# Cross-attention of a decoder layer: block transposes on VectorE with a trip through device memory in place of TensorE's transposes

## The chip, the cores and the metric

One NeuronCore of a Trainium2 chip runs the whole program. The metric is device time in microseconds from launch to end, the median of the runs. TensorE is called PE, VectorE DVE, ScalarE ACT, GpSimd POOL; SyncE (SP) only issues DMAs here.

## The reference

A decoder layer over 8 batch rows of 128 positions and 512 features, all in float32: causal self-attention, cross-attention and a linear layer, each with a residual and a layer norm ahead of it. The change touches the cross-attention, for each batch row b (the linear layer follows it row by row):

```python
kv = jnp.concatenate([context, latents], axis=1)          # 256 rows, 512 wide
q = latents @ Wq      # 32 heads of 128
k = kv @ Wk           # 8 heads of 128
v = kv @ Wv
q, k = rms_norm(q, q_norm_w), rms_norm(k, k_norm_w)
scores = einsum('bhgqd,bhkd->bhgqk', qg, k) / sqrt(128)   # four query heads to a key head
out = einsum('bhgqk,bhkd->bhgqd', softmax(scores), v)
return out @ Wo
```

The linear layer's weights come as 4-bit values with a scale per group and are unpacked on the chip.

## The kernel before

Products are made in float32r from split operands: a value is a high part (`hi`, rounded) plus a low part (`lo`, the rest), and `split_matmuls` (L76) issues three matmuls (hi x hi, lo x hi, hi x lo) for each block of 128 in the contraction. So every operand of a product needs a copy (mostly on ACT) for its high part and a subtraction (mostly on DVE) for its low part.

First comes `self_attention`, to about 249 us of the span. It leaves the rows in `x` (the accumulator `acc`), their normalised transposes `xT`, the context's transposes `cT`, the first set of weights, and the products of the first step in `ps_kv` and `ps_q`. `cross_attention_and_linear` then runs 64 steps s = 8 j + b: for each of the 8 key heads j (with its four query heads) the 8 batch rows b. The order of the work is written out by hand as one list for each engine, with semaphores between them. The bodies of j = 0 and j = 7 are written out, those between are a hardware loop.

A step does this. PE: `scores` (12 matmuls of 256 columns into `ps_s0`, `ps_s1`); `project_keys_values` for the next step (24 of 256 into `ps_kv`); `project_queries` for the next step (12 of 512 into `ps_q`); `probs_transposed` (8 transposes of 128x128 of p, L1210, into two banks `ps_pT`); `queries_keys_transposed` for the next step (4 transposes into `ps_q`, L1216, and 2 into `ps_kv`, L1221); `project_output` of the step before (12 of 512 into `ps_y`); `values` (6 of 512 into `ps_o`). DVE: the maxima over the scores and the bias of the exponential (`biases`), the scaling of p by the inverse of its total (`probs`, L1055), `v_lo`, the normalised keys `k_sb`, the low parts `pT_lo` (two), `qT_lo`, `kT_lo`, `oT_lo`, and the residual. ACT: four exponentials with their totals, the sums of squares for both rms norms, a copy `q_sb` of the queries, and the high parts. The rms of the queries isn't applied to them but to the scores, as the scale of the exponential. POOL: the two chains that turn sums of squares into inverse roots (`rms`, L882 and L884), and the low parts of the weights (`weights_low`, L876).

Weights of a key head: `wkv`, `wq` and `wo`, one buffer each for the raw array, the high and the low part. The high and low parts of the next head's `wkv` and `wq` are made in step b = 6, once the products of this head are issued, those of `wo` in b = 0. SP loads the raw arrays as they come free.

PSUM's eight banks are all in use: two for scores, two for the transposes of p, and `ps_q`, `ps_kv`, `ps_o`, `ps_y`. After the last step the linear layer's rows follow, each with statistics, norm, transposes, product and store.

## Time and profile before

| | |
|---|---|
| Median of 3 runs | 1114.6 us (1114.39 to 1115.09) |
| Profiled execution, its own time | 1114.33 us |
| Its span | 1112.2 us |
| Mean granted PE clock over the span | 0.982 of full speed |
| Busy in the span | PE 1050.4, DVE 757.1, ACT 611.9, POOL 358.5 us |
| DMA | 31.73 MB moved, mean 29 GB/s |
| First and last scores of the cross-attention | 253.7 and 1070.9 us |

The span runs from the first to the last instruction that the profiler recorded. Matmuls are pipelined, so the mean of one (395 ns for 512 columns) is longer than the distance at which they follow each other; the chain of waits shows that distance. Busy times of engines run side by side and don't add up.

### The profile page before, as it was taken

To read this page: it belongs to the slowest core of one execution; us is meant where nothing else is said; L and a number is where in the kernel's file an instruction comes from. 1 tells how busy PE (TensorE), PEld (TensorE's weight loads), DVE (VectorE), ACT (ScalarE), POOL (GpSimd) and SP (SyncE) were. 2 spreads that over 40 slices of the span, in tenths; PEclk is the share of its full clock that TensorE was granted. 3 is DMA by queue.
4 is the path that set the end of the run, shared out by engine and by line. 5 is a ranking of instruction groups with operands and counts; after the bars stand their busy time and mean duration, and the time that the engine had idled before them with its cause. 6 is when DMAs were issued, how large, how long until landed. Compare 5 with 4: busy or idle time off the path is not lost.

```text
span 1112.2 us, 19358 instructions
## 1 busy us (share of the span) xinstructions
PE 1050.4 (94%) x6436; PEld 902.8 (81%) x6436; DVE 757.1 (68%) x1561; ACT 611.9 (55%) x2324; POOL 358.5 (32%) x460
## 2 busy tenths in 40 slices
PE   6788888778999999999999999999999999999998
PEld 5666666547888888888888888888888888888886
DVE  6788888756557756665666576657666665667774
ACT  2666666525555655555555555555555555555551
POOL 4622333033114312431432143114313331433443
PEclk9899999878999999999999999999999999999999
DMA  5000010003001100110011011001100110010002
GB/s 180 21 10 9 9 66 10 1 3 126 6 1 58 39 1 2 57 38 0 19 38 38 0 57 38 0 0 57 38 0 0 57 38 0 11 37 1 1 1 76
DMA packets 8935, 31.73 MB, mean 29 GB/s; under 512 B 1600, under 2 KB 1600, under 8 KB 6720
## 3 DMA queue, kind: packets, MB, share of 16 engines
q1 hardware_dynamic: 8896, 31.23, 8.0%
q8 instruction: 22, 0.36, 0.1%
q14 instruction: 17, 0.14, 0.0%
HBM read 29.13 MB, written 2.10 MB: 28 GB/s over the span
## 4 chain that ended last, share of the span: by engine, by line
PE 64%; POOL 7%; DVE 3%; ACT 2%; issue 1%; POOLq 0%; DVEq 0%
PE ps_q L76 15%; PE ps_y L76 14%; PE ps_kv L76 13%; PE ps_s L76 7%; PE ps_o L76 7%; PE ps_pT L1210 4%; POOL wq_lo L876 3%; POOL wkv_lo L876 2%; PE ps_q L1216 2%; ACT p L957 1%; PE ps_kv L1221 1%; POOL q_rms L884 1%; DVE neg_max L1042 1%; POOL k_rms L884 1%; DVE wkv_hi L1035 0%
## 5 line engine op out<-in xcount | busy, mean ns | idle before, releaser
L957 ACT ACTIVATE p<-ps_s,bias,q_rms 128x256 f32<-128x256 f32 x256 | 141.3, 560 | 117.1 <-DVE bias L1046 116.3
L1068 DVE TENSOR_TENSOR pT_lo<-ps_pT,pT_hi 128x512 fp32r<-128x512 f32 x128 | 82.5, 686 | 75.6 <-ACT pT_hi L983 75.4
L993 ACT ACTIVATE oT_hi<-ps_o 128x512 fp32r<-128x512 f32 x64 | 38.3, 598 | 139.2 <-PE ps_o L76 139.2
L882 POOL TENSOR_TENSOR k_rms<-k_mean,rms_eps 128x2 f32<-128x2 f32 x64 | 19.6, 306 | 283.9 <-ACT k_squares L964 283.9
L76 PE MATMUL ps_y<-wo_hi,oT_hi 128*128 128x512 f32 x256 | 106.5, 416 | 0.0
L76 PE MATMUL ps_q<-wq_hi,xT_hi 128*128 128x512 f32 x256 | 101.1, 395 | 2.5 <-POOL wq_lo L876 2.5
L76 PE MATMUL ps_q<-wq_hi,xT_lo 128*128 128x512 f32 x256 | 101.9, 398 | 0.0
L76 PE MATMUL ps_y<-wo_hi,oT_lo 128*128 128x512 f32 x256 | 101.4, 396 | 0.0
L76 PE MATMUL ps_q<-wq_lo,xT_hi 128*128 128x512 f32 x256 | 100.9, 394 | 0.0
L76 PE MATMUL ps_y<-wo_lo,oT_hi 128*128 128x512 f32 x256 | 100.7, 393 | 0.0
L971 ACT ACTIVATE q_sb<-ps_q 128x512 f32<-128x512 f32 x64 | 38.3, 599 | 100.8 <-PE ps_q L76 99.5
L882 POOL TENSOR_TENSOR q_rms<-q_mean,rms_eps 128x4 f32<-128x4 f32 x64 | 13.5, 210 | 245.2 <-ACT q_squares L976 245.2
L1085 DVE TENSOR_TENSOR oT_lo<-ps_o,oT_hi 128x512 fp32r<-128x512 f32 x64 | 44.2, 691 | 69.3 <-ACT oT_hi L993 69.3
L1055 DVE TENSOR_SCALAR p<-p,inv 128x256 f32<-128x256 f32 x256 | 86.5, 380 | 4.5
L1042 DVE TENSOR_REDUCE neg_max<-ps_s 128x2 f32<-128x512 f32 x128 | 87.5, 684 | 2.2 <-PE ps_s L76 2.2
L1081 DVE TENSOR_TENSOR x<-ps_y,x 128x512 f32<-128x512 f32 x64 | 44.3, 691 | 62.3 <-PE ps_y L76 62.3
L976 ACT ACTIVATE q_squares<-q_sb 128x128 f32<-128x128 f32 x256 | 77.3, 334 | 0.0
L76 PE MATMUL ps_s<-kT_hi,qT_hi 128*128 128x256 f32 x256 | 72.7, 284 | 1.2 <-DVE kT_lo L1076 1.2
L76 PE MATMUL ps_kv<-wkv_lo,cT_hi 128*128 128x256 f32 x256 | 73.4, 287 | 0.0
L76 PE MATMUL ps_kv<-wkv_hi,cT_lo 128*128 128x256 f32 x256 | 73.2, 286 | 0.0
L76 PE MATMUL ps_kv<-wkv_hi,cT_hi 128*128 128x256 f32 x256 | 73.0, 285 | 0.0
L76 PE MATMUL ps_s<-kT_hi,qT_lo 128*128 128x256 f32 x256 | 72.7, 284 | 0.0
(210 smaller groups left out, 3316.1 us busy)
## 6 DMA issues: line engine op xcount, KB each, us to landing
raw_wq<-in_x_wq SPq DMA_DIRECT2D x8, 1024.0 KB, 4.8
raw_wo<-in_x_wo SPq DMA_DIRECT2D x8, 1024.0 KB, 4.9
raw_wkv<-in_x_wkv SPq DMA_DIRECT2D x8, 512.0 KB, 3.3
ctx_raw<-in_ctxT SPq DMA_DIRECT2D x8, 256.0 KB, 2.6
out<-raw_wq SPq DMA_DIRECT2D x8, 256.0 KB, 2.0
x<-in_x SPq DMA_DIRECT2D x1, 1536.0 KB, 9.8
raw_wq<-in_a_wq SPq DMA_DIRECT2D x2, 512.0 KB, 6.0
raw_wq<-in_a_wo SPq DMA_DIRECT2D x1, 1024.0 KB, 4.7
```

What stands on the lines that cost most here:

```text
L76: mm = pe.matmul(out, lhsT, rhs, start=start and i == 0, stop=stop and i == len(terms) - 1)
L876: i = pool.tensor_tensor(w[1][:, c, :], raw[:, c, :], f32(w[0][:, c, :]), ALU.subtract)
L957: act.activation(p[:, g, :], ps_s[g // 2][:, g % 2 * KV:(g % 2 + 1) * KV], ACT.Exp, bias=bias[:, g:g + 1], scale=q_rms[:, g:g + 1], accum_ ...
L971: act.activation(q_sb[:], ps_q[:].rearrange("p (g d) -> p g d", g=XG), ACT.Copy).then_inc(q_ok, 1)
L976: i = act.activation(q_squares[:, g, :], q_sb[:, g, :], ACT.Square, scale=XD ** -0.5, accum_out=q_mean[:, g:g + 1])
L993: act.activation(oT[0][:], ps_o[:].rearrange("p (g s) -> p g s", g=XG), ACT.Copy).then_inc(o_hi, 1)
L1042: dve.tensor_reduce(neg_max[:, two], ps_s[h][:].rearrange("p (g k) -> p g k", g=2), AX.X, ALU.max, negate=True).then_inc(max_ok, 1)
L1055: i = dve.tensor_scalar(p[:, g, :], p[:, g, :], inv[:, g:g + 1], None, ALU.mult)
L1068: dve.tensor_tensor(pT[1][:, t], ps_pT[t][:].rearrange("p (g s) -> p g s", g=XG), f32(pT[0][:, t]), ALU.subtract).then_inc(pT_lo, 1)
L1081: dve.tensor_tensor(acc[:, b, :], ps_y[:], acc[:, b, :], ALU.add).then_inc(acc_ok, 1)
L1085: dve.tensor_tensor(oT[1][:], ps_o[:].rearrange("p (g s) -> p g s", g=XG), f32(oT[0][:]), ALU.subtract).then_inc(o_lo, 1)
L1210: mm = pe.transpose(ps_pT[t][:, g * S:(g + 1) * S], p[:, g, t * S:(t + 1) * S], ident[:])
```

## The change

The 14 transposes of a step leave PE. For p, for the raw queries and for the normalised keys there is instead:

1. `dve.transpose`, which transposes each 32x32 block and leaves the blocks where they are put (`p_blocks`, 1024 columns in two instructions; `qk_blocks`, 768 columns in two: the queries straight from `ps_q`, the keys from `k_sb`);
2. one DMA on SP's queue that stores the blocks to a scratch array in device memory (512 KB for p, 384 KB for queries and keys), with a wait for it;
3. four DMAs that load them back, each into 32 partitions (a quadrant j of the transposed array), in runs of 1024 bytes for p and 768 for queries and keys (`pT_raw`, `qk_raw`). The scratch arrays are double, as is `pT_raw`; `p_blocks`, `qk_blocks` and `qk_raw` are single.

High and low parts are made from these arrays in SBUF: `pT_hi` and `qT_hi`, `kT_hi` on ACT; `pT_lo` (in place, one instruction of 1024 columns) and `qT_lo` on POOL; `kT_lo` on DVE. The copy `q_sb` is gone: the squares are read from `ps_q`, and the arrays of squares are bf16 now.

The pipeline is deeper: in iteration s PE issues the scores of s, the keys, values and queries of s + 2, the output of s - 2 and the values of s - 1, in this order. `v` has four buffers, `q_rms` four. The other engines' lists follow. All 64 steps are written out; there is no hardware loop.

`wq` and `wkv` (high and low) are double, so the next head's are made earlier: `wkv_hi` at b = 0, `wo_hi` at 1, `wq_hi` at 2 on DVE; the low parts on POOL in pieces of two blocks at b = 2, 3 (`wkv`), 4, 5 (`wq`) and 1 (half of `wo`; DVE makes the other half). The first set of `wq` serves as the linear layer's weights. The linear layer has two banks of its own (`ps_xn`, `ps_f`, those of `ps_pT`) and starts in the last two iterations: its rows 0 to 3 are issued there, the rest between the last products.

The core of the diff:

```diff
-        wq, wkv, wo = mem["wq"], mem["wkv"], split("wo", [P, XG, D])
+        wq = [mem["wq"], split("wq1", [P, C, D])]
+        wkv = [mem["wkv"], split("wkv1", [P, C, NKV])]
+        wo = split("wo", [P, XG, D])
...
+        qk_blocks = sb("qk_blocks", [P, 4, XG + 2, R])
+        qk_raw = sb("qk_raw", [P, 4, XG + 2, R])
...
-        v = [split(f"v{i}", [P, 2, XD]) for i in range(2)]
+        v = [split(f"v{i}", [P, 2, XD]) for i in range(4)]
...
-        pT = split("pT", [P, 2, XG, S])
+        p_blocks = sb("p_blocks", [P, 8, XG, R])
+        pT_hi_sb = sb("pT_hi_sb", [P, 4, 2, XG * R], F32R)
+        pT_raw = [sb(f"pT_raw{i}", [P, 4, 2, XG * R], F32R) for i in range(2)]
...
+            def queries_keys(s):
+                sp.wait_ge(k_blocked, s + 1)
+                sp.wait_ge(q_blocked, s + 1)
+                wait(sp, qT_lo, s)
+                scratch = io["qk_scratch"][s % 2]
+                sp.dma_start(scratch, qk_blocks[:].rearrange("p j x c -> p (j x c)")).then_inc(qk_stored, 16)
+                wait(sp, kT_lo, s)
+                sp.wait_ge(qk_stored, 16 * (s + 1))
+                quadrants = scratch.rearrange("(i r) (j x) -> j r i x", i=4, j=4)
+                for j in range(4):
+                    sp.dma_start(qk_raw[R * j:R * j + R].rearrange("p i x c -> p i (x c)"), quadrants[j]).then_inc(qk_loaded[s % 4], 16)
+            def probs(s):
+                sp.wait_ge(p_blocked, 2 * s + 2)
+                if s >= 2:
+                    sp.wait_ge(pT_lo, s - 1)
+                scratch = io["p_scratch"][s % 2]
+                sp.dma_start(scratch, p_blocks[:].rearrange("p m g c -> p (m g c)")).then_inc(p_stored, 16)
+                if s >= 2:
+                    sp.wait_ge(o_ps, s - 1)
+                sp.wait_ge(p_stored, 16 * (s + 1))
+                quadrants = scratch.rearrange("(i r) (j x) -> j r i x", i=4, j=4)
+                for j in range(4):
+                    sp.dma_start(f32(pT_raw[s % 2][R * j:R * j + R].rearrange("p i t x -> p i (t x)")),
+                                 quadrants[j]).then_inc(p_loaded[s % 4], 16)
...
+            for s in range(STEPS):
+                j, b = divmod(s, B)
+                if s + 1 < STEPS:
+                    queries_keys(s + 1)
+                probs(s)
+                if b == 3 and j < LAST:
+                    sp.wait_ge(wo_lo, j + 1)
+                    sp.wait_ge(wo_lo_dve, j + 1)
+                    load(raw_wo, "x_wo", wo_in, j + 1)
+                if b == 4 and j + 2 < XKVH:
+                    sp.wait_ge(wkv_lo, 2 * j + 2)
+                    load(raw_wkv, "x_wkv", wkv_in, j + 2)
+                if b == 6 and j + 2 < XKVH:
+                    sp.wait_ge(wq_lo, 2 * j + 2)
+                    load(raw_wq, "x_wq", wq_in, j + 2)
...
+            def queries_low(s):
+                pool.wait_ge(qT_hi, s + 1)
+                pool.tensor_tensor(qT[1][:].rearrange("p g (i c) -> p g i c", i=4),
+                                   qk_raw[:, :, 0:XG, :].rearrange("p i g c -> p g i c"),
+                                   f32(qT[0][:]).rearrange("p g (i c) -> p g i c", i=4), ALU.subtract).then_inc(qT_lo, 1)
+
+            def probs_low(s):
+                pool.wait_ge(pT_hi, s + 1)
+                raw = pT_raw[s % 2][:].rearrange("p i t x -> p (i t x)")
+                pool.tensor_tensor(raw, f32(raw), f32(pT_hi_sb[:].rearrange("p i t x -> p (i t x)")),
+                                   ALU.subtract).then_inc(pT_lo, 1)
...
+            for s in range(STEPS):
+                j, b = divmod(s, B)
+                if j < LAST and b in (2, 3):
+                    weights_low(wkv[(j + 1) % 2], raw_wkv, (2 * b - 4, 2 * b - 3), wkv_hi, wkv_lo, j + 1)
+                if j < LAST and b in (4, 5):
+                    weights_low(wq[(j + 1) % 2], raw_wq, (2 * b - 8, 2 * b - 7), wq_hi, wq_lo, j + 1)
+                if s:
+                    probs_low(s - 1)
+                if s + 2 < STEPS:
+                    k_rms_step(s + 2)
+                if s + 1 < STEPS:
+                    queries_low(s + 1)
+                if b == 1:
+                    weights_low(wo, raw_wo, (2, 3), wo_hi, wo_lo, j + 1)
+                if s + 2 < STEPS:
+                    q_rms_step(s + 2)
+                if j == LAST:
...
             def probs_high(s):
-                for t in range(2):
-                    act.wait_ge(pT_ps, 2 * s + t + 1)
-                    act.activation(pT[0][:, t], ps_pT[t][:].rearrange("p (g s) -> p g s", g=XG), ACT.Copy).then_inc(pT_hi, 1)
+                act.wait_ge(p_loaded[s % 4], landed(s))
+                act.activation(pT_hi_sb[:], f32(pT_raw[s % 2][:]), ACT.Copy).then_inc(pT_hi, 1)

             def queries_keys_high(s):
-                act.wait_ge(qT_ps, s + 1)
-                act.activation(qT[0][:], ps_q[:].rearrange("p (g d) -> p g d", g=XG), ACT.Copy).then_inc(qT_hi, 1)
-                act.wait_ge(kT_ps, s + 1)
-                act.activation(kT[0][:], ps_kv[:, 0:KV], ACT.Copy, scale=key_scale[:, 0:1]).then_inc(kT_hi, 1)
+                act.wait_ge(qk_loaded[s % 4], landed(s))
+                act.activation(kT[0][:].rearrange("p (i t c) -> p i t c", i=4, t=2), qk_raw[:, :, XG:, :], ACT.Copy,
+                               scale=key_scale[:, 0:1]).then_inc(kT_hi, 1)
+                act.activation(qT[0][:].rearrange("p g (i c) -> p g i c", i=4),
+                               qk_raw[:, :, 0:XG, :].rearrange("p i g c -> p g i c"), ACT.Copy).then_inc(qT_hi, 1)

...
+            keys_values(0)
+            query_sums(0)
+            keys_values(1)
+            query_sums(1)
+            queries_keys_high(0)
+            for s in range(STEPS):
+                j, b = divmod(s, B)
+                if s >= 2:
+                    output_high(s - 2)
                 exps(s)
...
+                if s:
+                    probs_high(s - 1)
+                if s + 2 < STEPS:
+                    keys_values(s + 2)
+                if s + 1 < STEPS:
                     queries_keys_high(s + 1)
...
+                if s + 2 < STEPS:
+                    query_sums(s + 2)
...
+            def probs(s, h):
+                two = slice(2 * h, 2 * h + 2)
+                dve.wait_ge(exp_done, 2 * s + h + 1)
+                dve.reciprocal(inv[:, two], total[:, two]).then_inc(inv_ok, 1)
+                dve.wait_ge(inv_ok, 2 * s + h + 1)
+                for g in range(2 * h, 2 * h + 2):
+                    i = dve.tensor_scalar(p[:, g, :], p[:, g, :], inv[:, g:g + 1], None, ALU.mult)
+                i.then_inc(p_ok, 1)
+                wait(dve, p_stored, 16 * s)
+                dve.wait_ge(p_ok, 2 * s + h + 1)
+                dve.transpose(p_blocks[:, :, two, :], p[:, two, :].rearrange("p g (m r) -> p m g r", r=R)).then_inc(p_blocked, 1)
...
+            def keys_blocked(s):
                 dve.wait_ge(k_rms_ok, s + 1)
                 dve.tensor_tensor(k_sb[:], kv_rows[:, :, 0:XD], k_rms[:].unsqueeze(2).broadcast_to([P, 2, XD]),
                                   ALU.mult).then_inc(k_ok, 1)
...
+                wait(dve, qk_stored, 16 * s)
+                dve.wait_ge(k_ok, s + 1)
+                dve.transpose(qk_blocks[:, :, XG:, :].rearrange("p j x c -> p x j c"),
+                              k_sb[:].rearrange("p t (j r) -> p t j r", r=R)).then_inc(k_blocked, 1)
...
+            def queries_blocked(s):
+                dve.wait_ge(q_ps, s + 1)
+                wait(dve, qk_stored, 16 * s)
+                dve.transpose(qk_blocks[:, :, 0:XG, :].rearrange("p j x c -> p x j c"),
+                              ps_q[:].rearrange("p (g j r) -> p g j r", g=XG, r=R)).then_inc(q_blocked, 1)
...
+            def keys_low(s):
                 dve.wait_ge(kT_hi, s + 1)
+                dve.scalar_tensor_tensor(kT[1][:].rearrange("p (i t c) -> p i t c", i=4, t=2), qk_raw[:, :, XG:, :],
+                                         key_scale[:, 0:1], f32(kT[0][:]).rearrange("p (i t c) -> p i t c", i=4, t=2),
+                                         ALU.mult, ALU.subtract).then_inc(kT_lo, 1)
...
+            for s in range(2):
+                queries_blocked(s)
+                values_low(s)
+                keys_blocked(s)
+            keys_low(0)
+            for s in range(STEPS):
+                j, b = divmod(s, B)
                 biases(s)
...
+                if s >= 2:
+                    output_low(s - 2)
+                probs(s, 0)
+                probs(s, 1)
+                if s + 2 < STEPS:
+                    values_low(s + 2)
+                if s + 1 < STEPS:
+                    keys_low(s + 1)
+                if s + 2 < STEPS:
+                    keys_blocked(s + 2)
+                    queries_blocked(s + 2)
+                if s >= 2:
+                    residual(s - 2)
+                if b == 1:
+                    output_weights(j)
+                if j < LAST and b == 0:
+                    weights_high(wkv[(j + 1) % 2], raw_wkv, wkv_in, j + 1, wkv_hi)
+                if j < LAST and b == 2:
+                    weights_high(wq[(j + 1) % 2], raw_wq, wq_in, j + 1, wq_hi)
...
+            def values(s):
+                pe.wait_ge(pT_lo, s + 1)
+                wait(pe, o_lo, s)
+                hi, lo = pT_hi_sb, pT_raw[s % 2]
+                split_matmuls(pe, ps_o[:], [(v[s % 4][0][:, t, :], v[s % 4][1][:, t, :], hi[:, :, t, :], lo[:, :, t, :])
+                                            for t in range(2)]).then_inc(o_ps, 1)
+
...
+            project_keys_values(1)
+            project_queries(1)
+            for s in range(STEPS):
+                j, b = divmod(s, B)
...
                 scores(s)
...
+                if s + 2 < STEPS:
+                    project_keys_values(s + 2)
...
+                if s + 2 < STEPS:
+                    project_queries(s + 2)
+                if s >= 2:
+                    project_output(s - 2)
...
+                if s:
+                    values(s - 1)
+            xn_transposed(4)
...
-    nc = bacc.Bacc("TRN2", target_bir_lowering=False, num_devices=1)
+    nc = bacc.Bacc("TRN2", target_bir_lowering=False, num_devices=1, dynamic_dma_scratch_size=4096)
...
+    io["p_scratch"] = [nc.dram_tensor(f"p_scratch{i}", (P, XG * KV), F32, kind="Internal").ap() for i in range(2)]
+    io["qk_scratch"] = [nc.dram_tensor(f"qk_scratch{i}", (P, (XG + 2) * XD), F32, kind="Internal").ap() for i in range(2)]
```

## Rows read from the trace of the kernel before

**Rows 1.** Window table: us, busy (instructions) per engine, granted PE clock, DMA share, GB/s.

```profile
400.00:450.00 50.00, 50.00 (x310) 44.15 (x309) 30.70 (x72) 28.57 (x108) 14.34 (x22) 1.00 0.03 12
```

**Rows 2.** Chain of waits, one step: start us, us, engine, tile, line, instructions.

```profile
410.20 1.42 PE ps_s L76 x12
411.62 2.88 PE ps_kv L76 x24
414.50 2.80 PE ps_q L76 x12
417.30 0.87 PE ps_pT L1210 x8
418.18 0.47 PE ps_q L1216 x4
418.65 0.22 PE ps_kv L1221 x2
418.87 2.79 PE ps_y L76 x12
421.66 1.40 PE ps_o L76 x6
```

**Rows 3.** Waits: engine line <- releaser: us in total, times, longest.

```profile
PE ps_q L76 <- POOL wq_lo L876: 2.5, 7, 0.4
```

**Rows 4.** Chain of waits, start of the cross-attention and end of the program.

```profile
251.25 0.44 DVE k_sb L1062
...
253.66 2.90 PE ps_s L76 x12
...
1085.80 2.82 PE ps_y L76 x12
...
1109.01 0.69 DVE raw_wq L1130
```

**Rows 5.** DMA issues of the page (KB each, us to landing); SP's timeline (start, us).

```profile
raw_wq<-in_x_wq SPq DMA_DIRECT2D x8, 1024.0 KB, 4.8
...
raw_wkv<-in_x_wkv SPq DMA_DIRECT2D x8, 512.0 KB, 3.3
...
out<-raw_wq SPq DMA_DIRECT2D x8, 256.0 KB, 2.0
...
447.22 0.33 SPq L840 DMA_DIRECT2D raw_wkv<-in_x_wkv  x1
```

**Rows 6.** Groups by line: shapes, count | busy us, mean ns | idle before, releaser.

```profile
L1042 DVE TENSOR_REDUCE neg_max<-ps_s 128x2 f32<-128x512 f32 x128 | 87.5, 684 | 2.2 <-PE ps_s L76 2.2
L1055 DVE TENSOR_SCALAR p<-p,inv 128x256 f32<-128x256 f32 x256 | 86.5, 380 | 4.5
L1068 DVE TENSOR_TENSOR pT_lo<-ps_pT,pT_hi 128x512 fp32r<-128x512 f32 x128 | 82.5, 686 | 75.6 <-ACT pT_hi L983 75.4
L1046 DVE TENSOR_TENSOR bias<-neg_max,q_rms 128x2 f32<-128x2 f32 x128 | 44.7, 349 | 4.9
...
L1035 DVE CAST wq_hi<-raw_wq 128x2048 fp32r<-128x2048 f32 x7 | 8.6, 1227 | 0.0
...
L957 ACT ACTIVATE p<-ps_s,bias,q_rms 128x256 f32<-128x256 f32 x256 | 141.3, 560 | 117.1 <-DVE bias L1046 116.3
```

**Rows 7.** Timeline of VectorE and GpSimd around a weight switch: start us, us, instruction.

```profile
448.26 5.02 POOL L876 TENSOR_TENSOR wq_lo<-raw_wq,wq_hi 128x512 fp32r<-128x512 f32 x4
450.77 1.29 DVE L1046 TENSOR_TENSOR bias<-neg_max,q_rms 128x2 f32<-128x2 f32 x1
...
464.31 0.16 DVE L1046 TENSOR_TENSOR bias<-neg_max,q_rms 128x2 f32<-128x2 f32 x1
```

**Rows 8.** Groups of GpSimd by line, columns as in rows 6.

```profile
L884 POOL TENSOR_TENSOR q_rms<-q_rms,minus_half 128x4 f32<-128x4 f32 x64 | 64.4, 1007 | 5.0
...
L876 POOL TENSOR_TENSOR wkv_lo<-raw_wkv,wkv_hi 128x256 fp32r<-128x256 f32 x28 | 26.9, 988 | 8.0 <-DVE wkv_hi L1035 8.0
...
L927 POOL TENSOR_TENSOR f_w_lo<-raw_wo,f_w_hi 128x1024 fp32r<-128x1024 f32 x2 | 4.8, 2404 | 0.0
```

More of the change, by code:

```diff
@@ L1174, in _, with project_keys_values @@
+            statistics(6)
+            normalised(6)
+            out_row(4)
+            out_row(5)
+            output_low(STEPS - 1)
+            xn_low_row(6)
+            residual(STEPS - 1)
+            statistics(7)
+            normalised(7)
+            out_row(6)
+            xn_low_row(7)
+            out_row(7)
         @block.tensor
         def _(pe):
[L1176 to L1180 removed]
+            def project_keys_values(s):
+                j, b = divmod(s, B)
+                wait(pe, v_lo, s)
+                wait(pe, k_ok, s)
+                wait(pe, wkv_lo, 2 * j)
+                rows, weight = slice(b * S, (b + 1) * S), wkv[j % 2]
```

443 lines of the change are left out of this document (180 added, 263 removed).

## The prediction, made before the changed kernel ran

> **What bounds the kernel now.** I read the window table first, then the chain of waits, then the groups of instructions by line. In the window table [rows 1] the reader sees TensorE (PE) busy for all of a 50 us stretch of the cross-attention at a granted clock of 1.00 (the 2.4 GHz level), beside VectorE (DVE) 30.7, ScalarE (ACT) 28.6 and GpSimd (POOL) 14.3 us, with the DMA engines almost idle. The chain in the same stretch [rows 2] is one head step of TensorE and nothing else: 1.42 + 2.88 + 2.80 + 0.87 + 0.47 + 0.22 + 2.79 + 1.40 = 12.85 us. So a step costs what TensorE issues in it, and there are 64. The reader should note the three short pieces (L1210, L1216, L1221): 14 transposes, 0.87 + 0.47 + 0.22 = 1.56 us per step. The self-attention before it, up to about 249 us, is not touched.
>
> **What the change takes off TensorE.** All 14 transposes: 64 x 1.56 = 99.8 us. The other 66 matmuls of a step stay as they are, 11.29 us. The second set of weights also removes the wait for the low half of the query weights, 2.5 us in 7 switches [rows 3]. The query product stands ahead of the output product in the old step too (414.50 and 418.87 in [rows 2]), so that order moves nothing; what moves is the distance: products for step s+2, values of s-1 and output of s-2 stand in step s now. TensorE's time is the same, and a result may be one step later before anyone waits.
>
> **Start.** Before, the normalised keys of step 0 are ready at 251.25 + 0.44 = 251.7 and the first scores start at 253.66 [rows 4]. After, between the two stand: a block transpose (0.4), a store of 384 KB, four loads, the high halves (two ACT instructions, about 1.1), the low half of the queries on POOL (1.29, priced below). The nearest DMAs [rows 5]: 256 KB stored 2.0 us, 512 KB loaded 3.3, 1024 KB loaded 4.8, so 1.5 us per further 512 KB. Estimate: store 2.0 + 0.4 = 2.4 plus the issue; the loads, issued one behind the other at 0.33 each, 3.3 at the least (as one load of 512 KB) and 1.0 + 4.8 = 5.8 at the most (from the last issue, at the price of twice the bytes, should loads into 32 partitions at a time run at half the rate). I take 4.2, near the lower end, since the bytes decide. The first scores come at about 262, 8.3 late; but the key/value and query products of step 1 (2.88 + 2.80) are done in that gap, so net +2.6. The first p needs its own trip, and the first two steps have nothing else to fill: about 5 us of gaps. **End.** After the last output product before, 1088.6, the chain runs to 1109.0 through five more rows of the linear layer [rows 4]; after the change those rows mostly stand ahead of it. They are moved, not removed; only the idle of the statistics chain, about 4 us, is partly filled: -1. Together -2.5 + 2.6 + 5 - 1 = +4.
>
> **The best case** is thus 1112.2 - 99.8 + 4 = 1016.4 of span; with the 2.1 us around it (the profiled execution took 1114.3) 1018.5. The median of the three shown, 1114.6, is 0.3 above that execution, which is nothing here.
>
> **What has to fit under 11.29 us a step.** Three loops come close to that, and each is priced by its nearest rows.
>
> *VectorE.* Per step [rows 6]: two maxima with their bias (2 x (0.68 + 0.16)), four scalings of p (4 x 0.38), two reciprocals (0.3), `oT_lo` and the residual (2 x 0.69), and three passes of 256, `v_lo`, `kT_lo` and `k_sb` (3 x 0.44, by `k_sb` in [rows 4]). Gone are `pT_lo` twice and `qT_lo`, 3 x 0.69 = 2.06. New are four block transposes: p twice 512 columns, queries 512, keys 256. No row shows one. A pass of 512 columns takes 0.68 in every form seen from PSUM and a fast scaling 0.38 for 256, so the bounds are about 0.4 and 1.4 (twice the pass) for 512; I take 0.68 and 0.42, the pass they are nearest to: 2.5 in all. Sum 8.7; with the weight copies (1.23 for 2048 columns: two of these, one of half the width and the new half subtraction come to about 0.5 as a mean over eight steps) 9.2 of 11.29, between 8.3 and 11.8. That fits, alone.
>
> The Trainium skill (page VectorE: DVE Perf Modes, section The three transpose paths) gives 311 ns for a 128x128 block transpose in bf16, and the 32x32 blocks only. Taken four times for 512 columns that would be 1.24 us and VectorE's sum 11.1 rather than 9.2; taken as a fixed part and one column per cycle it would be my value. No row here can tell which.
>
> *The port that VectorE and GpSimd share.* The row that speaks against this change is the bias of 128x2: 0.16 us in an ordinary step, and 1.29 at 450.77, while POOL is inside its group of four subtractions [rows 7]; it ended where one of these ended. Where POOL works from SBUF, the small instruction waits for it. In the new kernel POOL has such work in every step: `queries_low`, 512 columns, 1.29 us, and `probs_low`, 1024 columns in one instruction, 2.40 [rows 8]. With the two rms chains (2.2, of which the power for the queries alone is 1.01) and the low halves of the weights ((4 x 0.99 + 6 x 1.29)/8 = 1.5) POOL is busy for 7.4 us of a step, against 3.7 (14.34/50 of 12.85) now. `probs_low` starts when ACT has made `pT_hi`, right after the exponentials, just where VectorE scales the second half of p. If the last scaling waits for it, that costs up to 2.4; if `kT_lo`, now read from SBUF, meets `queries_low`, up to 1.3. VectorE's sum is then 12.9 at worst and 9.2 at best. VectorE has about 1.1 us per step of waits for the exponentials (560 ns each [rows 6]) and the rms that can overlap these, so I put its loop at 10.5 to 12.
>
> The Trainium skill (page SBUF — State Buffer, section Who interferes with whom) says that the pair is an exclusive lock held for the whole instruction. By that rule the 2.4 us instruction is worse than the four of 1.29 seen here, and a VectorE that always meets it is at 12.9.
>
> *SP and the trips.* SP waits for each store before it issues the loads, and both trips go through its one queue. Trip of p: 2.75 (store of 512 KB) + 4 x 0.33 = 4.1; trip of q and k: 2.4 + 1.3 = 3.7; 7.8 at the least. A store queued behind the loads before it waits for their bytes, up to 1.5 each, and the weights (2.5 MB in eight steps, 0.9 us per step) go through the same rings: 7.8 + 3.0 + 0.9 = 11.7 at the most. I take 10. The traffic, 1.8 MB per step, is about 160 GB/s plus the weights. As latency: p blocked about 6.4 us into its step, its trip 2.75 + 0.33 + 4.2 = 7.3, ready 13.7 after the scores started; ACT takes it up in the next step after that step's exponentials, at 15.3. So p has some 1.6 us of slack, the keys and queries about 1.5.
>
> **Forecast.** The three loops lie close to TensorE's 11.29 and each has steps in which it is longer: weights on POOL in four of eight steps, copies on VectorE in three, loads of 1 MB or 512 KB ahead of a trip in three. I expect no stall in about half the steps and some 0.8 us in the others, 0.4 as a mean: 64 x 0.4 = 25. 1018 + 25 = **1043 us**, TensorE about 96% busy, a step of 11.7.
>
> **Rivals.** (1) *A loop binds, but below the old step.* The scalings wait for `probs_low` in nearly every step, or SP's queue is full: 12.2 us a step, 1018 + 64 x 0.9 = 1076 (1062 to 1105). For it: the 1.29 us bias row, and sums that reach 12.9 and 11.7. Against it: VectorE now has 19 us of waits in 50, and these waits can overlap. (2) *The other side: the round trip closes a loop longer than the old step.* From q blocked to `kT_hi` and on to the next q blocked stand store 2.75, loads 4.2, ACT 0.5 to 1.1, `kT_lo` 0.5, `k_sb` and its transpose 0.9, the q transpose 0.7: 9.6 to 10.2. If trips take 3.5 us more than I think (loads at the 5.8 end, and a store that waits behind them), this is 13.6 per step: 1018 + 64 x 2.3 = 1165, slower. It decides from 1.5 us of stall per step on ((1114.3 - 1018.5)/64), that is a step of 12.8. For it: nothing in the trace shows a load into 32 partitions in runs of 768 bytes. Against: slack in three places and a DMA share of 0.03 now. (3) *Nothing stalls*: 1018, if `probs_low` happens to fall into VectorE's waits. It differs from the forecast in size only.
>
> **How the numbers follow.** Forecast with rival 3 as its lower end (1012 to 1062): 0.53. Rival 1: 0.27. Rival 2: 0.17. Between them, within 0.2% of no change (2.2 us, about what a measurement of this kernel can tell): 0.03. So faster 0.80, same 0.03, slower 0.17. The range takes the first two whole, and leaves out rival 2: 1012 to 1105.
>
> **What will show it.** TensorE rows of steady steps: no transposes, a step of 11.3 where nothing stalls; wrong if the matmuls themselves became slower. The block transposes near 0.68 for 512 columns; at 1.2 VectorE binds. The mean of the p scaling (0.38 now) and of the bias (0.35 now) would rise with the port: over 0.8 for the scaling says rival 1. TensorE's waits by releaser: `qT_lo` or `kT_lo` ahead of the scores speak for the trip of q and k, `pT_lo` ahead of the values for that of p, `k_sb` or the blocked queries ahead of the products for VectorE. The forecast is wrong if a trip takes over 9 us from store to last load, or if VectorE's busy share comes over 90%.

## The result, and the profile after

The changed kernel takes 1168.3 us (median, 1165.5 to 1170.7) against 1114.5 for the kernel before on the same chip (1111.7 to 1115.1): ratio 1.049, 95% interval 1.046 to 1.052. It is slower by 54 us where 1043 was forecast.

The head of the page of the kernel after, with its chain of waits by share, and its DMA issues (KB each, us to landing):

```profile
span 1164.9 us, 18100 instructions
PE 991.7 (85%) x5523; PEld 835.0 (72%) x5540; DVE 863.9 (74%) x1633; ACT 577.3 (50%) x2196; POOL 573.8 (49%) x572
...
DVE 24%; DMA 21%; PE 14%; SPq 8%; issue 5%; POOL 3%; ACT 3%; DVEq 0%; POOLq 0%; ACTq 0%
...
p_scratch<-p_blocks SPq DMA_DIRECT2D x64, 512.0 KB, 2.6
pT_raw<-p_scratch SPq DMA_DIRECT2D x256, 128.0 KB, 3.0
qk_scratch<-qk_blocks SPq DMA_DIRECT2D x64, 384.0 KB, 3.5
qk_raw<-qk_scratch SPq DMA_DIRECT2D x256, 96.0 KB, 2.2
raw_wq<-in_x_wq SPq DMA_DIRECT2D x8, 1024.0 KB, 7.0
```

TensorE has 14% of the chain. VectorE, DMA and SP's queue (SPq) have 53% together. The window table answers to [rows 1] (us; busy time of PE, PEld, DVE, ACT, POOL; granted TensorE clock; DMA share; GB/s), here for the kernel after:

```profile
400.00:450.00 50.00, 43.99 (x239) 37.37 (x238) 40.48 (x73) 25.40 (x95) 31.07 (x33) 0.97 0.51 161
...
300.00:1000.00 700.00, 629.13 (x3512) 546.11 (x3513) 528.08 (x1038) 360.36 (x1334) 386.61 (x387) 0.95 0.53 166
```

TensorE stands still for 6 us in 50. Over 300 to 1000 us its granted clock is a mean of 0.95, where the kernel before had 1.00 (the 2.4 GHz level) in the same stretch. The groups that answer to [rows 6, 8] (mean ns of one behind the busy us):

```profile
L1132 DVE TENSOR_SCALAR p<-p,inv 128x256 f32<-128x256 f32 x256 | 157.9, 658 | 4.5
L940 POOL TENSOR_TENSOR pT_raw<-pT_raw,pT_hi_sb 128x1024 fp32r<-128x1024 f32 x64 | 157.4, 2459 | 157.4 <-ACT pT_hi_sb L1045 157.4
...
L1136 DVE STREAM_TRANSPOSE p_blocks<-p 128x512 f32<-128x512 f32 x128 | 91.1, 712 | 13.3
L1121 DVE TENSOR_REDUCE neg_max<-ps_s 128x2 f32<-128x512 f32 x128 | 87.8, 686 | 46.2 <-PE ps_s L76 45.9
...
L1159 DVE SCALAR_TENSOR_TENSOR kT_lo<-qk_raw,key_scale,kT_hi 128x256 fp32r<-128x256 f32 x64 | 45.7, 714 | 123.0 <-ACT kT_hi L1049 122.9
...
L1154 DVE STREAM_TRANSPOSE qk_blocks<-ps_q 128x512 f32<-128x512 f32 x64 | 43.3, 676 | 7.9 <-PE ps_q L76 7.4 <-PEq L88 0.3
...
L1124 DVE TENSOR_TENSOR bias<-neg_max,q_rms 128x2 f32<-128x2 f32 x128 | 40.6, 318 | 4.4
...
L1148 DVE STREAM_TRANSPOSE qk_blocks<-k_sb 128x256 f32<-128x256 f32 x64 | 28.5, 446 | 6.7
```

The block transposes cost what was put in. The same scaling of `p` takes 658 ns instead of 380.

**Where the time went.** The distance between the first maxima (`neg_max`) of one step and the next, read off VectorE's timeline, is the length of a step (64 steps in all, eight to a head); the place is `b`, the step's number within its head. The means over heads 1 to 6, in us:

```
place b           0      1      2      3      4      5      6      7     head
before        12.86  12.86  12.86  12.86  12.86  12.86  12.86  13.46    103.5
after         12.25  12.51  13.17  11.29  17.18  12.68  11.28  14.27    104.6
```

At places 3 and 6 a step is 11.28 to 11.29, TensorE's own work, as forecast. The rest stalls: 14.4 us a head over 8 x 11.28, 1.8 a step and not 0.4. So the 12.6 us that the transposes freed in each head are all spent. The 52.7 us by which the span grew divide so: the first maximum comes at 269.2 instead of 255.3 (+14); the seven heads 0 to 6 take 730.2 instead of 725.6 (+5); the last head's seven steps 112.9 instead of 91.7 (+21), one of them 25.6; from the last maximum to the end 52.6 instead of 39.7 (+13).

The 17.18 at place 4 in the chain of waits of the kernel after (start us, us, what):

```profile
523.57 2.62 DMA p_scratch<-p_blocks
...
528.08 0.38 SPq L844
...
528.56 8.65 DMA qk_scratch<-qk_blocks
...
538.59 2.47 DMA qk_raw<-qk_scratch
...
541.49 0.62 ACT qT_hi L1051
...
542.18 1.28 POOL qT_lo L933
...
543.50 2.93 PE ps_s L76 x12
```

L844 issues the 1 MB load of `raw_wo`; the 384 KB store of the blocked queries and keys is issued 0.48 us behind it and lands after 8.65 us. A step earlier (store at 515.70, first load behind it at 519.05) it took under 3.35. The store is late by 5.3 and the scores wait. So it is every time in the heads 0 to 6: from the store to the first of its loads back, SP needs 6.7 to 8.7 us behind each of the 13 loads of 1 MB and 5.4 to 5.9 behind each of the six of 512 KB. The waits of the engines say the same (line <- releaser: us in total, times, longest; kernel after):

```profile
ACT kT_hi L1049 <- DMA qk_raw<-qk_scratch: 170.7, 53, 9.0
...
PE ps_s L76 <- POOL qT_lo L933: 86.9, 37, 6.7
...
SPq L854 <- DMA qk_scratch<-qk_blocks: 265.7, 63, 8.3
```

The 12.3 to 13.2 of places 0 to 2 are in VectorE's list. Its chain, and GpSimd's and VectorE's timelines beside it (start us, us; kernel after):

```profile
505.85 0.63 DVE p L1132 x2
...
507.37 2.99 DVE p L1132 x2
...
511.47 1.22 DVE kT_lo L1159
```

```profile
507.74 2.45 POOL L940 TENSOR_TENSOR pT_raw<-pT_raw,pT_hi_sb 128x1024 fp32r<-128x1024 f32 x1
```

The first pair of scalings takes 0.63, the second 2.99, and it ends about when `probs_low` does (510.36 against 510.19).

### The profile page after: what moved, and what is told of

Read it like the earlier page. It is cut to its first block, busy times and chain, and to the rows that moved or that the text cites. A ratio compares the mean times of both kernels' runs of the same rounds, so it can differ in the third digit from the quotient of the medians.

```text
span 1164.9 us, 18100 instructions
## 1 busy us (share of the span) xinstructions
PE 991.7 (85%) x5523; PEld 835.0 (72%) x5540; DVE 863.9 (74%) x1633; ACT 577.3 (50%) x2196; POOL 573.8 (49%) x572
## 4 chain that ended last, share of the span: by engine, by line
DVE 24%; DMA 21%; PE 14%; SPq 8%; issue 5%; POOL 3%; ACT 3%; DVEq 0%; POOLq 0%; ACTq 0%
DMA qk_scratch<-qk_blocks 12%; DVE p L1132 8%; DMA p_scratch<-p_blocks 6%; PE ps_s L76 4%; SPq L871 4%; DMA qk_raw<-qk_scratch 3%; DVE p_blocks L1136 3%; DVE neg_max L1121 3%; PE ps_q L76 3%; SPq L857 3%; PE ps_kv L76 3%; PE ps_y L76 2%; DVE bias L1124 2%; POOL qT_lo L933 2%; DVE oT_lo L1170 1%
## 5 line engine op out<-in xcount | busy, mean ns | idle before, releaser
L940 POOL TENSOR_TENSOR pT_raw<-pT_raw,pT_hi_sb 128x1024 fp32r<-128x1024 f32 x64 | 157.4, 2459 | 157.4 <-ACT pT_hi_sb L1045 157.4
L1132 DVE TENSOR_SCALAR p<-p,inv 128x256 f32<-128x256 f32 x256 | 157.9, 658 | 4.5
L76 PE MATMUL ps_s<-kT_hi,qT_hi 128*128 128x256 f32 x256 | 81.9, 320 | 86.9 <-POOL qT_lo L933 86.9
L1039 ACT ACTIVATE q_squares<-ps_q 128x128 bf16<-128x128 f32 x256 | 67.4, 278 | 148.4 <-DVE qk_blocks L1154 148.4
L1159 DVE SCALAR_TENSOR_TENSOR kT_lo<-qk_raw,key_scale,kT_hi 128x256 fp32r<-128x256 f32 x64 | 45.7, 714 | 123.0 <-ACT kT_hi L1049 122.9
L933 POOL TENSOR_TENSOR qT_lo<-qk_raw,qT_hi 128x512 fp32r<-128x512 f32 x64 | 81.9, 1279 | 100.1 <-ACT qT_hi L1051 99.5
L76 PEld LDWEIGHTS ps_s<-kT_hi,qT_hi 128*128 128x128 f32 x256 | 53.7, 210 | 104.4 <-POOL qT_lo L933 103.1
L1049 ACT ACTIVATE kT_hi<-qk_raw,key_scale 128x256 fp32r<-128x256 f32 x64 | 32.7, 511 | 170.7 <-DMA qk_raw<-qk_scratch 170.7
L1136 DVE STREAM_TRANSPOSE p_blocks<-p 128x512 f32<-128x512 f32 x128 | 91.1, 712 | 13.3
L76 PE MATMUL ps_s<-kT_lo,qT_hi 128*128 128x256 f32 x256 | 77.8, 304 | 0.0
```

The source lines that it names most:

```text
L76: mm = pe.matmul(out, lhsT, rhs, start=start and i == 0, stop=stop and i == len(terms) - 1)
L933: pool.tensor_tensor(qT[1][:].rearrange("p g (i c) -> p g i c", i=4), qk_raw[:, :, 0:XG, :].rearrange("p i g c -> p g i c"), f32(qT[0][:]) ...
L940: pool.tensor_tensor(raw, f32(raw), f32(pT_hi_sb[:].rearrange("p i t x -> p (i t x)")), ALU.subtract).then_inc(pT_lo, 1)
L1039: i = act.activation(q_squares[:, g, :], ps_q[:, g * XD:(g + 1) * XD], ACT.Square, scale=XD ** -0.5, accum_out=q_mean[:, g:g + 1])
L1049: act.activation(kT[0][:].rearrange("p (i t c) -> p i t c", i=4, t=2), qk_raw[:, :, XG:, :], ACT.Copy, scale=key_scale[:, 0:1]).then_inc(k ...
L1132: i = dve.tensor_scalar(p[:, g, :], p[:, g, :], inv[:, g:g + 1], None, ALU.mult)
```

## The experiments

Each ratio is to the kernel before, whose runs were made beside it, with its 95% interval. "Places" are step lengths by `b` as above. Line numbers in fences are those of each kernel.

**What stalls the steps: the weights' loads, GpSimd, the end, the start.** Five kernels, each of which undoes one suspect.

`x1_light`: the weights of later heads are loaded as 16 numbers a partition; the rest of them stays that of an earlier head.

```diff
+            def load_light(raw, name, sem, j):
+                sp.dma_start(raw[:, 0, 0:16], io[name][j][:, 0:16]).then_inc(sem, 16)
...
-                    load(raw_wo, "x_wo", wo_in, j + 1)
+                    load_light(raw_wo, "x_wo", wo_in, j + 1)
```

(The other two loads likewise.)

> The weight loads of later heads are cut to 16 elements per partition (8 KB each), so later heads compute with stale weights; all waits, copies and low parts stay. Theory A (a 1 MB or 512 KB load issued right ahead of the store of queries and keys delays that trip): the three long steps of a head (17.2, 12.7 and 14.3 us in the changed kernel) fall to 11.3 to 11.8, 10 us per head, 7 heads: about 1098 us. Rival B (VectorE waits for GpSimd on the shared port): these loads were hidden, the steps stay, at most 10 us come back: 1158 or more. Rival C (each trip is too long by itself): the same as B.

Measured 1107.5, ratio 0.994 (0.991 to 0.997): 61 us less than after, where 70 was expected. Place 4 falls from 17.18 to 12.07, place 7 from 14.27 to 11.52; SP issues as many DMAs as before, so it is the bytes that cost and not the issues. The loads are the largest part; places 1 and 2 stay at 12.40 and 13.15.

`x2_split`: `probs_low` in four instructions of 256 columns.

```diff
-                pool.tensor_tensor(raw, f32(raw), f32(pT_hi_sb[:].rearrange("p i t x -> p (i t x)")),
-                                   ALU.subtract).then_inc(pT_lo, 1)
+                high = pT_hi_sb[:].rearrange("p i t x -> p (i t x)")
+                for c in range(4):
+                    part = slice(256 * c, 256 * (c + 1))
+                    i = pool.tensor_tensor(raw[:, part], f32(raw[:, part]), f32(high[:, part]), ALU.subtract)
+                i.then_inc(pT_lo, 1)
```

> The low part of p on GpSimd is made in four instructions of 256 columns in place of one of 1024. Theory B (port): the mean of the scaling of p falls from 0.66 to about 0.45 us and the steps b = 0, 1, 2 of a head, bound by VectorE, lose 0.5 to 1.5 us each: 15 to 30 us in all, 1138 to 1153 us; the last head, where the scaling waits 3 to 4 us, gives more. Theory A: the steps behind the weight loads stay long, 17.2 and 14.3. If the four instructions run back to back without letting VectorE in, nothing changes: 1168.

Measured 1144.3, ratio 1.028 (1.023 to 1.034), 24 less. The scaling in this kernel's groups:

```profile
L1135 DVE TENSOR_SCALAR p<-p,inv 128x256 f32<-128x256 f32 x256 | 116.6, 497 | 4.5
```

497 ns, between 380 and 658. At 505 us of its timeline a pair of scalings takes 1.10 beside GpSimd's group of four (2.98): VectorE waits for one piece, not for the group.

`x3_tail`: the first linear rows stand behind the last scores instead of ahead of them.

```diff
+                scores(s)
                 if j == LAST and b == 7:
+                    linear(0)
                     xn_transposed(2)
+                    linear(1)
                     xn_transposed(3)
-                scores(s)
...
-                    linear(2 * b - 12)
-                    linear(2 * b - 11)
+                    if b == 7:
+                        linear(2)
+                        linear(3)
```

> The first two rows of the linear layer and the transposes of rows 2 and 3 are issued behind the scores of the last step, not ahead of them. Theory D (the last scores wait for the chain of the norm, a step of 25.6 us): the scores of step 63 start 12 to 15 us earlier; part comes back because the linear rows are then late, so 6 to 12 us are gained: 1156 to 1162 us. Rival: the end is set by the last trip of p and the rows behind it in any case: 1168.

Measured 1155.1, ratio 1.039 (1.035 to 1.043), 13 less; the step of 25.6 falls to 16.8. The profiled execution took 1169.8, more than the other four (1152.8 to 1157.9), so its trace shows the step but not the gain: its last head is 10 us shorter and its heads 0 to 6 are 7 longer than in the kernel after.

`x4_start`: step 0's queries pass ahead of step 1's sums and rms, in ACT's, POOL's and VectorE's lists.

```diff
             keys_values(1)
+            queries_keys_high(0)
             query_sums(1)
-            queries_keys_high(0)
```

(ScalarE's list; the other two are changed to match.)

> At the start of the cross-attention the high and low parts of the queries of step 0 are made ahead of the sums of squares and the rms of step 1. Theory E (the first scores wait in GpSimd's and ScalarE's queues behind step 1, 267.4 in place of the 262 that I forecast): the first scores start 4 to 5 us earlier and all follows: 1164 us. Rival: the trip of step 1 then sets the pace and nothing is left of it: 1168.

Measured 1165.9, ratio 1.048 (1.041 to 1.055): nothing that can be told from after. The first maximum comes at 259.4 instead of 269.2; the maximum of step 8 is 6.4 ahead, that of step 16 only 2.4, and the last 2.4. An early start runs into the same loops, which give it back.

`x5_no_low`: the low part of `p` is made for 16 of its 1024 columns only.

```diff
-                pool.tensor_tensor(raw, f32(raw), f32(pT_hi_sb[:].rearrange("p i t x -> p (i t x)")),
-                                   ALU.subtract).then_inc(pT_lo, 1)
+                high = pT_hi_sb[:].rearrange("p i t x -> p (i t x)")
+                pool.tensor_tensor(raw[:, 0:16], f32(raw[:, 0:16]), f32(high[:, 0:16]), ALU.subtract).then_inc(pT_lo, 1)
```

> The changed kernel with the low part of p made for 16 of 1024 columns only, so the product of the values uses the full p as low part in the rest. Theory B (port): the scaling of p returns to 0.38 us, the steps b = 0 to 2 to the sum of VectorE's list, and more is gained than with the four instructions: 1130 to 1142 us. The steps behind the weight loads stay at 14 to 17 us, so it doesn't come below 1120.

Measured 1120.9, ratio 1.007 (1.004 to 1.010): 47 less, more than forecast. Places 0 to 2 are 11.92, 12.11 and 10.97, which gives back 2.9 of their 4.1 us over TensorE's work; places 4 and 7 stay at 16.32 and 13.92. The scaling is at 378 ns, its old 380 [rows 6], so the long instruction accounts for all of its rise. Twice x2's gain leaves room for something else that the instruction held up; `w4_order_only` below looks for it.

**Small pieces of weights.** `y1_pieces` loads the same bytes in 256 and 128 KB pieces, each behind the loads of queries and keys and ahead of the store of `p`. `y2_parts` is that with x2 and x3; `y3_spread` adds the spreading of the 16 scale loads over three steps; `y4_casts` adds the high halves of `wkv` and `wq` on ScalarE.

```diff
+                if b in (2, 3, 4, 5) and j < LAST:
+                    piece(raw_wo, "x_wo", wo_in, j + 1, b - 2)
...
                 probs(s)
...
-                    load(raw_wo, "x_wo", wo_in, j + 1)
```

> All the weights are loaded, in pieces of 256 or 128 KB spread over the steps, each issued behind the loads of queries and keys and ahead of the store of p. Theory A (it is the place and the size of a load in SP's queue, not the bytes, that costs): as with the tiny loads, 1100 to 1115 us, the steps b = 4, 5, 7 at 11.3 to 12.5. Rival F (the bytes cost wherever they stand, since the DMA engines are short): those steps share out the same loss, 1145 or more. Rival G: the store of p behind them is late and the values wait for p: PE waits for pT_lo ahead of ps_o of more than 20 us in all.

> The pieces, the low part of p in four instructions, and the linear rows behind the last scores, together. If the three losses are independent, about 60 + 24 + 11 us off 1168: 1065 to 1080, below the kernel before. If the port and the loads hide each other, 1090 to 1100.

> As y2_parts, and the 16 loads of the linear layer's scales, which SP issues in a row for 7.6 us between two trips, are spread over three steps. Theory A: the step of 18 us at the start of the last head falls to 12.5 to 13.5, 5 us less than y2_parts. Rival: no difference.

> As y3_spread, and ScalarE makes the high parts of wkv and wq in place of VectorE. Theory B (VectorE's list is what binds the steps b = 0, 1, 2): they lose 0.7 and 1.2 us, 7 heads: about 10 us less than y3_spread. Rival: ScalarE's copy of 2048 columns (about 2 us) delays the sums of squares and the exponentials, and nothing is gained.

```
                median   ratio (95%)                place 0 to 7
y1_pieces       1130.4   1.017 (1.013 to 1.020)     12.06 14.17 13.17 11.19 12.31 12.64 13.07 11.96
y2_parts        1110.7   0.998 (0.996 to 1.000)     12.17 14.22 12.33 10.96 11.97 12.40 12.77 12.11
y3_spread       1107.3   0.994 (0.992 to 0.997)     12.13 14.03 12.29 10.97 12.10 12.52 12.75 12.31
y4_casts        1106.1   0.994 (0.990 to 0.997)     11.86 14.28 11.49 11.62 12.46 12.68 12.52 12.35
```

The pieces give 38 of x1's 61. At places 4, 5 and 7 together they give 7.2 us a head, against 8.4 in x1; what they lack stands mostly at places 0, 1 and 6. The expectations of y1, y2 and y4 are missed. In y3 step 56 falls from 17.97 to 14.34, where 12.5 to 13.5 was expected. In y4 places 0 and 2 do lose 0.3 and 0.8, but places 3 to 5 grow by as much together, and in place of 10 us less there is 1, which can't be told from y3. So most steps stay near 12.3, whatever is taken off VectorE. In y4's chain of waits:

```profile
444.79 4.19 DMA p_scratch<-p_blocks
...
449.41 0.70 SPq L903
...
451.17 3.08 DMA qk_scratch<-qk_blocks
...
456.08 0.43 SPq L847
456.62 4.15 DMA p_scratch<-p_blocks
```

SP's own list is now the loop: store of `p`, wait, four loads (L903), store of queries and keys, wait, four loads, a piece (L847), the next store of `p` after 11.83 us. Behind the piece the store of `p` takes 4.2, where it took 2.6 in the kernel after. Place 1, at 14.0 to 14.3 in all four, is longer still: there y4's chain (474.58 to 493.88) leaves SP after the loads of queries and keys and goes through VectorE's list, with the copy `wo_hi` (1.14) in it.

**SP's order.** `z1_swap` is y4 with the two trips beside each other in SP's list: store of `p`, store of q and k, loads of `p`, loads of q and k. `z2_swap_only` is the changed kernel with that swap alone, `z3_swap_y3` is y3 with it.

```diff
                     queries_keys(s + 1)
+                if s:
+                    load_probs(s - 1)
+                if s + 1 < STEPS:
+                    load_queries_keys(s + 1)
                 probs(s)
```

(`queries_keys` and `probs` issue only their stores now.)

> As y4_casts, and SP issues the store of the next queries and keys ahead of the loads of p, so the store no longer queues behind their bytes and its latency lies beside their issue. Theory H (in y4_casts SP's own list is what binds: store of p 4.2, four issues 1.75, store of q and k 3.3, four issues 1.75, a piece 0.45: 11.5 to 11.9 us a step): SP's list shrinks to about 10 us, steps of 11.5 on the mean, 1070 to 1085 us. Rival (VectorE binds): the steps stay near 12.3, 1100 or more.

> The changed kernel with this exchange in SP's list alone. Here the big weight loads still stand ahead of the trips, behind the loads of p and ahead of nothing else: theory A, extended: a weight load now stands ahead of the store of p and no longer ahead of that of q and k... the load follows the loads of q and k, so the long steps 17.2 and 14.3 become 12 to 14: about 1120 to 1140 us. Rival H alone: a gain of at most 1 us per step in the short steps, 1150 or more.

> As z1_swap with the weight copies on VectorE (y3_spread and the exchange). Theory H: 1075 to 1090 us; z1_swap is lower by 5 to 10 us once SP no longer binds, since then VectorE's list does in the steps b = 0 and 2.

z1 1137.1 (1.024, 1.021 to 1.026), z2 1130.9 (1.018, 1.015 to 1.021), z3 1130.8 (1.017, 1.015 to 1.020). The swap takes some 35 off the changed kernel (0.031 of 1114) and *adds* about 32 to y4 (0.030), where 1070 to 1085 was expected; z3 was expected at 1075 to 1090.

z2's time is as expected, and its profile shows why the loads cost so much in the kernel after. The weights are still loaded whole there and still stand ahead of the store of queries and keys (the expectation says otherwise), but SP now issues them right behind the store of `p` and not behind its loads back, so 4.1 to 6.5 us ahead of the store of queries and keys instead of 0.5:

```profile
505.96 0.38 SPq L844 DMA_DIRECT2D raw_wo<-in_x_wo  x1
510.73 0.32 SPq L852 DMA_DIRECT2D qk_scratch<-qk_blocks  x1
...
513.35 1.73 SPq L860 DMA_DIRECT2D qk_raw<-qk_scratch  x4
```

The store has landed after 2.62 at most. Over the 19 such stores of the heads 0 to 6 it is 2.6 to 4.4, where it was 5.4 to 8.7. The places are 12.59, 14.11, 13.14, 11.37, 12.64, 12.30, 12.33 and 12.06: the long steps at 4 and 7 are gone with every byte and every whole load still there. So it is the distance between load and store that decides. Some 0.7 of the difference is the swap's own: its stores no longer stand right behind the loads of `p`, and their median falls from 3.3 in x1, which has no weights to wait for either, to 2.6.

What the swap costs, one turn of z1's chain of waits shows:

```profile
506.64 3.92 DMA pT_raw<-p_scratch
...
510.58 1.07 ACT pT_hi_sb L1074
...
511.72 3.01 POOL pT_raw L969 x4
...
514.96 0.71 POOL k_rms L949
515.69 0.44 DVE k_sb L1181
...
516.59 0.69 DVE qk_blocks L1191
...
517.33 0.32 SPq L884
...
519.24 4.68 DMA pT_raw<-p_scratch
```

The loads of `p` now wait for the blocked queries and keys, those for `k_rms`, and `k_rms` stands behind the low part of `p` in GpSimd's list, which needs the loads of `p`. A loop of 12.4 to 13.3 us. The same loop is in z2's chain.

**GpSimd's and ScalarE's order.** The keys' squares ahead of `pT_hi` on ScalarE, `k_rms` ahead of the low part of `p` on GpSimd: in y4 (`w1_order`), in z1 (`w2_order_swap`), in the changed kernel alone (`w4_order_only`); `w3_wo_late` is w2 with `q_rms` ahead of GpSimd's half of `wo_lo`.

```diff
+                if s + 2 < STEPS:
+                    k_rms_step(s + 2)
                 if s:
                     probs_low(s - 1)
-                if s + 2 < STEPS:
-                    k_rms_step(s + 2)
```

(GpSimd's list; on ScalarE `keys_values(s + 2)` likewise goes ahead of `probs_high(s - 1)`.)

> As y4_casts, with the sums of squares and the rms of the keys ahead of the high and low part of p in ScalarE's and GpSimd's lists. Theory H (SP's own list binds y4_casts): little changes, 1098 to 1106 us. Theory K (the loop over the low part of p and k_rms binds): 1070 to 1085.

> As z1_swap (1137 us) with that order. Theory K: the loop loads of p, pT_hi, low part, k_rms, k_sb, blocked queries, store is cut; both SP's list (10 us) and VectorE's are then below 12: 1065 to 1085 us, the best so far. Theory H has nothing to say against it. If VectorE still binds: 1100 or more.

> As w2_order_swap, with the rms of the queries ahead of GpSimd's half of the output weights. The step b = 1 (14.9 us in z1_swap) loses 1 to 2 us if that half delayed the chain: 7 to 14 us less than w2_order_swap. Rival: nothing, since that rms is needed two steps later.

> The changed kernel with the new order alone. The weight loads, the port and the end are as they were, so theories A and B leave 1155 to 1165 us; theory K would give 1140 or less.

```
                median   ratio (95%)                place 0 to 7
w1_order        1104.3   0.992 (0.989 to 0.995)
w2_order_swap   1060.7   0.953 (0.951 to 0.955)     11.35 12.26 11.62 11.59 11.44 11.41 11.28 11.43
w3_wo_late      1060.0   0.953 (0.951 to 0.955)
w4_order_only   1129.4   1.014 (1.011 to 1.017)     12.12 12.50 11.86 10.52 15.65 12.96 11.30 13.76
```

In w1 the order changes nothing that can be told from y4: SP's list is the loop there (in its chain over 450 to 500 us the two stores and SP's issues of the loads have 74%). In w2, where the swap has taken that away, the same order is worth some 78 us against z1 (0.071 of 1114); and the swap, which cost 32 in y4, is worth 44 against w1. In the changed kernel alone the order is worth 39 (1129.4, where the expectation was 1155 to 1165); w4's group

```profile
L1132 DVE TENSOR_SCALAR p<-p,inv 128x256 f32<-128x256 f32 x256 | 89.1, 390 | 4.5
```

is back at 390 ns: behind `k_rms`, the low part of `p` no longer meets the scalings (it meets `kT_lo` instead, 1175 ns against 714, where VectorE has idle time). So w4 does two things at once, it lets `k_rms` pass and keeps GpSimd's long instruction off the scalings, and no run here separates them. x2, which lets VectorE in and keeps the order, gave 24; what w4 and x5 gave beyond that can be the order's or the rest of the port's (in x2 a pair of scalings still takes 1.10 instead of 0.63). w3 finds nothing in `wo_lo`, where 7 to 14 was expected.

w2 beats both kernels: 1060.7, 50 below the 1111.0 of the original beside it. Its window table:

```profile
500.00:550.00 50.00, 49.60 (x299) 43.67 (x298) 37.33 (x85) 30.54 (x111) 31.27 (x41) 1.00 0.72 200
...
300.00:1000.00 700.00, 681.41 (x3941) 591.42 (x3940) 534.75 (x1167) 434.12 (x1512) 478.74 (x623) 1.00 0.64 184
```

TensorE is busy again at a granted clock of 1.00, at 92.4 us a head, with 200 GB/s moved beside it.

## Why the prediction was wrong, step by step

- **TensorE's part** held. The transposes are gone, and a step without a stall is 11.28.
- **The block transposes** held: 0.71 for 512 columns of `p`, 0.68 from PSUM, 0.45 for 256, against 0.68 and 0.42. The Trainium skill's 311 ns for 128 columns (VectorE: DVE Perf Modes, The three transpose paths), taken four times, would have been 1.24; this trace has 0.71, so the other reading, a fixed part and a part by columns, was right: by 446 ns for 256 columns and 712 for 512, both from SBUF, some 0.18 us and 1.04 ns a column.
- **The price of a trip** held. Store, then 1.3 us from the first to the fourth issue, then the fourth load's landing: for `p` 2.6 + 1.3 + 3.0 = 6.9 against 7.3; queries and keys, with no weights ahead, 3.35 + 1.3 + 2.2 = 6.9, as forecast. SP's turn without weights is 3.35 + 1.73 + 2.70 + 1.73 = 9.5, against 10.
- **The step that failed is "SP and the trips", in how it took the weights**: "0.9 us per step", a mean over eight steps of bytes. The loads do not come as a mean. One load of 1 MB stands 0.5 us ahead of one store of 384 KB and makes it 8.65 us long; the text's own slack for queries and keys was 1.5. The forecast did count three steps of eight with a load ahead of a trip, but put 0.8 us on a long step. Over the 11.28 of TensorE, places 4, 7 and 5 lose 5.9 + 3.0 + 1.4 = 10.3 us a head, of 14.4. The forecast's own sign of being wrong, a trip of over 9 us, came true there: from the store at 528.56 to the last load at 541.06 it is 12.5. So did its sign for the trip of queries and keys, TensorE's wait for `qT_lo` ahead of the scores. [Rows 5] had the 4.8 us in which 1 MB landed, from which the worst step could have been worked out. x1, y1 and z2 show it: of the 10.3 the first gives back 8.4 by taking the bytes away, the second 7.2 by place and size, the third 7.1 by moving whole loads some 4 to 6 us ahead of the store. The 23 us between x1 (-61) and y1 (-38) go with the bytes themselves or with the piece's turn in SP's list, which no run here separates. Nor does a run show why a store behind a load lands late, or what the loads would cost on another engine's queue.
- **VectorE with the port** was priced rightly by its ends (9.2 and 12.9) and wrongly in the middle: "10.5 to 12" had to be 12.3 to 13.2 at places 0 to 2, because `probs_low` met the second pair of scalings as feared, 2.99 us for 0.63. That is (12.25 + 12.51 + 13.17) - 3 x 11.28 = 4.1 us a head. x5 gives 2.9 of these back. It is rival 1's mechanism, though the mark set for it (a scaling above 0.8) wasn't reached, 0.66: the mean hides that only the second pair waits. The Trainium skill's exclusive lock (SBUF — State Buffer, Who interferes with whom) agrees with what the trace shows: one instruction of 2.45 holds VectorE for its length, four of 0.77 let it in between.
- **A chain was missing.** The forecast counted GpSimd's busy time (7.4 us of a step; 7.2 was measured, 386.6 us over the 53.5 steps of 300 to 1000) but not its order: `k_rms`, on the way to the next keys, stands behind `probs_low`, which waits for the trip of `p`. That the chain can bind is shown by z1 and w2: under the swap the order is worth some 78. In the changed kernel w4 puts the order and the port it frees together at 39 us.
- **Start.** The forecast had the first scores at 262; they start at 267.4, since step 0's low part of the queries stands behind step 1's `q_rms` in GpSimd's list. x4 shows that mending it alone gives nothing.
- **End.** "Moved, not removed", -1, was wrong: +21 in the last head and +13 behind it. Linear rows ahead of the last scores (x3: 13 us), the port again (3.86 us for a pair of scalings at 1094), and 16 small scale loads for which SP needs 7.64 us (spreading them, y3 over y2, gave 3 us, with intervals that overlap).
- **The rivals.** The mechanisms of rivals 1 and 2 are both there. Rival 2 gave the right side and nearly the time, 1165, by 3.5 us more in every trip; but the trips are not long, they are late in three steps of eight. Its own words "a store that waits behind them" name the cause. That its 1165 lies so near 1168.3 is luck: 34 of the 53 us by which the span grew stand in the last head and behind it, of which the rival says nothing.

The parts don't add: x1, x5, w4, y1, z2, x2 and x3 took 61, 47, 39, 38, 37, 24 and 13 (differences of medians) off a kernel that had 54 to give to break even, and combined they stopped at about 1106 until SP's order and GpSimd's order were changed together. How the shared time divides among them stays open, and with it why the step of 17.18 at place 4 falls to 15.65 in w4, 16.32 in x5 and 16.48 in x2, none of which moves a load; it falls to 12.1 to 12.6 in x1, y1 and z2, which do. w2 is still 42 above the best case of 1018.5. Its trace has 14.5 in heads 0 to 6 (646.2 us for 56 steps of 11.28), 11 in the last head (89.6 for seven), about 6 at the start (first maximum at 269.9) and the rest behind the last maximum, 54.6 us to the end where the kernel before had 39.7; apart from x3's change, which is in w2 too, no run worked on that end.

## What to carry to other kernels

Price an in-order DMA queue by its worst step: for each store or load that something waits for, what stands ahead of it, and how long that takes to land, against the slack; a mean of bytes per step says nothing. A large load needn't be cut for it: in z2 it was enough to issue it some 4 us or more ahead of the store instead of 0.5. Where an engine's list has a long instruction that waits for a far trip, put the short chain that doesn't depend on it ahead: here one call moved in each of two lists was worth 39 us alone and some 78 behind the swap. When loops of equal length stand side by side, taking one away shows the next, so a change that gives nothing, or a loss (the swap in z1), may be half of the one that pays: look at the chain again before it is dropped.

## What the runs showed of the hardware

- A 384 KB store issued 0.48 us behind a 1 MB load lands after 8.65 us, and under 3.35 without one (2.6, the median of z2, where the loads of `p` don't stand right ahead of it either). Issued 4.3 us or more behind a 1 MB load it has landed after 2.6 to 4.3 (z2). A 512 KB store goes from 2.6 to about 4.2 behind a 256 KB piece.
- The four loads of 32 partitions each cost SP 0.43 us an issue, 1.73 for four, not 0.33 as in [rows 5].
- With stalls of 1 to 6 us in most steps the granted clock is 0.95 over 300 to 1000 us (0.90 in two stretches of 50); with TensorE at 681 us busy of 700 it is 1.00. So a stall costs a little more than its own length: after TensorE had stood for 6.66 us, the scores behind it, 543.5 to 546.4, ran at a granted clock of 0.50, the 1.2 GHz level, and took 2.93 us instead of 1.42.
- GpSimd's subtraction in four parts is dearer by itself (770 ns a part, four in 2.98 us at 505 us of x2, against 2.46) and cheaper for the kernel.
